# Taking the router of a mixture layer from the first norm and the attended values, with picks in batches

## What is computed

```python
x = x + conv(gn(x))          # rfft over channels, 16 modes, mixed by weights, irfft
t = t + attn(ln(t))          # one head, causal, W_q, W_k, W_v, W_o 256 x 256
# ffn(ln(t)):
router_logits = flat_x @ router_w                    # 256 x 8
topk_w, topk_idx = top_k(softmax(router_logits), 2)  # then normalised to sum 1
for e in range(8):
    h = gelu(flat_x @ w_fc[e])                       # 256 x 1024
    out = out + combine[:, e:e+1] * (h @ w_proj[e])  # 1024 x 256
t = t + out
```

## Time and profile before

| | us |
|---|---|
| median of 3 runs | 723.77 (722.03 to 724.03) |
| profiled execution, its own time | 726.27 |
| span from first to last instruction | 724.5 |
| PE busy | 647.4 (89%) |
| DVE busy | 516.5 (71%) |
| POOL busy | 429.6 (59%) |
| ACT busy | 413.7 (57%) |
| mean granted clock of PE | 0.964 of full |

### The profile page before, as it was taken

How to read it: one execution, slowest core, us unless ns; L and a number is a source line. 1 busy time by engine, 2 the same in 40 slices (tenths; PEclk the granted TensorE clock), 3 DMA queues, 4 the chain that set the end, 5 groups by cost and what they waited for, 6 DMA issues and landing times. The chain is left out here.

```text
span 724.5 us, 16522 instructions
## 1 busy us (share of the span) xinstructions
PE 647.4 (89%) x5010; PEld 624.2 (86%) x5010; DVE 516.5 (71%) x1217; ACT 413.7 (57%) x703; POOL 429.6 (59%) x340
## 2 busy tenths in 40 slices
PE   0496999999940699999999999999999999999993
PEld 0385888888840599999999999999999999999993
DVE  8764577777764577787878777877787777777761
ACT  1804777766520556566666656565656565756550
POOL 5002326777666256766666666767676767676763
PEclk9999999999975799999999999999999999999998
DMA  8805752222323454433131313222222222232312
GB/s 343 273 0 186 276 179 74 92 90 97 106 105 113 136 162 146 96 108 59 29 59 31 57 31 57 41 47 45 43 49 39 51 37 52 36 53 35 57 19 29
DMA packets 39486, 64.13 MB, mean 89 GB/s; under 512 B 3808, under 2 KB 34848, under 8 KB 38304
## 3 DMA queue, kind: packets, MB, share of 16 engines
q0 software_dynamic: 14304, 18.92, 14.7%
q1 hardware_dynamic: 14816, 34.55, 13.5%
q10 hardware_dynamic: 10336, 10.31, 5.6%
HBM read 37.96 MB, written 25.81 MB: 88 GB/s over the span
## 5 line engine op out<-in xcount | busy, mean ns | idle before, releaser
L574 POOL TENSOR_TENSOR pj_lo<-w_ffn,pj_hi 128x1024 fp32r<-128x1024 f32 x78 | 189.1, 2425 | 122.8 <-ACT pj_hi L615 106.3
L1167 DVE TENSOR_TENSOR fc_lo<-w_ffn,fc_hi 128x1024 fp32r<-128x1024 f32 x78 | 116.1, 1527 | 86.2 <-ACT fc_hi L615 86.2
L564 POOL DMA_INDIRECT out<-y,add_id x78 | 121.9, 1563 | 45.1 <-issue 43.7
L615 ACT ACTIVATE pj_hi<-w_ffn 128x1024 fp32r x78 | 82.7, 1060 | 94.9 <-PE psO L1464 89.3
L615 ACT ACTIVATE fc_hi<-w_ffn 128x1024 fp32r x78 | 78.3, 1051 | 43.4 <-issue 43.4
L1464 PE MATMUL psP<-pj_hi,h_hi 128*128 128x256 f32 x312 | 91.5, 293 | 0.2 <-DVE h_lo L1167 0.2
L1464 PE MATMUL psP<-pj_hi,h_lo 128*128 128x256 f32 x312 | 88.5, 284 | 0.0
L1464 PE MATMUL psO<-pj_hi,h_lo 128*128 128x256 f32 x312 | 88.3, 283 | 0.0
L1464 PE MATMUL psO<-pj_lo,h_hi 128*128 128x256 f32 x312 | 88.3, 283 | 0.0
L1464 PE MATMUL psP<-pj_lo,h_hi 128*128 128x256 f32 x312 | 88.3, 283 | 0.0
L1464 PE MATMUL psO<-pj_hi,h_hi 128*128 128x256 f32 x312 | 88.1, 282 | 0.0
(11 more groups left out here) (252 smaller groups left out, 1639.4 us busy)
## 6 DMA issues: line engine op xcount, KB each, us to landing
w_ffn<-in_w_ffn SPq DMA_DIRECT2D x8, 2048.0 KB, 8.2
xg<-slots ACTq DMA_DIRECT2D x38, 265.0 KB
xc<-in_x_ch SPq DMA_DIRECT2D x4, 1024.0 KB, 8.9
out<-x SPq DMA_DIRECT2D x16, 256.0 KB
x<-in_x_tok SPq DMA_DIRECT2D x1, 3072.0 KB, 25.2
slots<-fill SPq DMA_DIRECT2D x9, 265.0 KB, 2.8
out<-y,add_id POOLq DMA_INDIRECT x78, 3.9
w_in<-in_w_in SPq DMA_DIRECT2D x1, 1024.0 KB, 13.7
```

The source lines that it names most:

```text
L564: nc.gpsimd.indirect_dma_start(out_d, bass.IndirectOffsetOnAxis(ap=add_id[:, s:s + 1], axis=0), y[:, s, :], None, compute_op=ALU.add).then ...
L574: nc.gpsimd.tensor_tensor(pj_lo[:, 4 * a:4 * a + 4, :], w_ffn[:, bass.ds(e, 1), (2 + a) * DFF:(3 + a) * DFF].rearrange("p a (c d) -> p (a ...
L615: nc.scalar.activation(out, src, ACT.Copy, **kw).then_inc(done, 1)
L1167: v.tensor_tensor(out, whole, upper.bitcast(F32), ALU.subtract).then_inc(done, 1)
```

## The change

It touches the opening, the attention stage and one input; the experts' stage stays as it is.

- **Router.** The second norm's input is x1 + attn, and the logits are linear in it up to the root. So `router_w`, with its column means taken away (`route_w`), is kept in 8 extra columns of `vo_w`, and its product with `vo_w` in 8 more (`riders`). The value products then have 272 columns: the attended values' product with 264 of them yields the attention part of the logits, and the last 8, times the root of variance of the first norm (`roots[..., 4:6]`, power 0.5), the part of x1 (`ride_in`). `logits_in` adds both. The logits are then right up to the factor of the second norm's reciprocal root, which changes no pick; `gap_scale` multiplies the difference of the two best by it before the exponential. The transposes of the second norm, ACT's copy of them (`router_in`) and `route` are gone.
- **Picks** go in batches of 4, 4, 2, 2, 2, 2 sequences, 8 or 4 tiles. The running count over tiles is one scan (`tensor_tensor_scan`) over expert-major columns in place of a chain of additions. `count_before` writes columns 384 on of `psP`.
- **Order.** Slots run from -2. The inverse DFT and `conv_out` run two sequences ahead; both norms of a slot share one variance, one root and one shift step, and the second norm's statistics and rows come one slot later. `shifts` of the slot before opens each DVE slot. POOL issues up to five scatters before the root of its slot (all that are ready from slot 16 on). ACT splits the upper parts of `spec` for two sequences at once, DVE the lower; `xn_t` and `v_b` have two buffers; the xn transposes use `psG`.
- **Opening.** Both folds, the column sums and a transposition of `vo_w` come before the first inverse DFT.

The diff, cut to its core: changed buffer declarations, slices by batch size, renamed semaphores and nearly all removed lines are left out (the removed ones stand in the functions above).

```diff
-PAIRS = B // 2
-EARLY_PAIRS = PAIRS - 2
-PT = NT // PAIRS
+BATCHES = (0, 4), (4, 4), (8, 2), (10, 2), (12, 2), (14, 2)
+BT = 2 * max(n for _, n in BATCHES)
+EARLY = 12
+RIDE = 2 * E
+VW = D + RIDE
+WHERE = 3 * P
...
+SLOTS = B + 6
...
+        def norms_in(k):
+            return (0 if on(k - 2) else 2), (4 if on(k + 2) else 2)
...
-            for k in range(-1, B + 6):
+            for k in range(-2, SLOTS - 2):
...
+            def root(k):
+                first, end = norms_in(k)
+                end += 2 if end == 4 else 0
+                pool.wait_ge(var_ready, k + 3)
+                nc.gpsimd.tensor_tensor(roots[:, k + 2, first:end], ve[:, first:end], power[:, first:end],
+                                        ALU.pow).then_inc(roots_ready, 1)
             def scatter(b, s, n):
+                j, t = batch_of(b), 2 * b + s
                 pool.wait_ge(xn2_ready, t + 1)
                 pool.wait_ge(weights_ready, j + 1)
                 pool.wait_ge(slot_ready, j + 1)
                 gate()
                 nc.gpsimd.indirect_dma_start(
+                    slots_d, bass.IndirectOffsetOnAxis(ap=slot[:, n, t:t + 1], axis=0), rows[:, t, :],
+                    None).then_inc(scattered_early if b < EARLY else scattered_ending, 16)
+            left = [(b, s, n) for b in range(B) for s in range(2) for n in range(PICKS)]
             def pool_slot(k):
+                room = 5 if k < B else len(left)
+                while left and room and k >= sum(BATCHES[batch_of(left[0][0])]) + 2:
+                    scatter(*left.pop(0))
+                    room -= 1
+                if on(k - 2) or on(k + 2):
+                    root(k)
...
-            for n, (w, bank) in enumerate(((qk_w, psS), (vo_w, psP))):
+            for n, (w, bank) in enumerate(((vo_w, psT1), (qk_w, psG))):
...
             def values(b):
                 act.wait_ge(v_mm, b + 1)
+                if b > 1:
+                    act.wait_ge(pv_mm, b - 1)
+                    act.wait_ge(ride_read, b - 1)
+                for s, bank in enumerate((psV, psT2)):
+                    copy(v_b[b % 2][:, s, :], bank[:, 0:VW], v_ready)
...
-                act.wait_ge(gap_ready, j + 1)
+                act.wait_ge(gap_scaled, j + 1)
...
+            def upper_spec(p):
+                if p > 1:
+                    act.wait_ge(idft_mm, 2 * p - 2)
+                this = spec[:, p * 2 * SEQ:(p + 1) * 2 * SEQ]
+                copy(spec_parts[0:MC, p % 2, :], this, spec_upper)
+                copy(spec_parts[MC:2 * MC, p % 2, :], this, spec_upper)
...
             def act_slot(k):
                 if on(k - 1):
                     softmax(k - 1)
+                for j in batch_at(k - 3):
                     pick_ratio(j)
                 if on(k):
                     keys_in(k)
+                if on(k + 1):
+                    if later(k + 1):
+                        act.wait_ge(t1_mm, k + 1)
+                    normalise(k + 1, k, 2, xn, xn_ready)
                 if on(k - 1):
                     probs_out(k - 1)
                 if on(k):
                     values(k)
                 if on(k + 1):
                     normed_in(k + 1)
+                if on(k - 3):
+                    normalise(k - 3, k, 0, rows[:, 2 * k - 6:2 * k - 4, :], xn2_ready)
+                if k % 2 == 0 and on(k + 4):
+                    upper_spec(k // 2 + 2)
+            act.wait_ge(vot_mm, 1)
+            copy(g_t[:, :, :], psT2[:, :], vot_ready)
+            act.wait_ge(spec_ready, WI)
+            upper_spec(0)
+            act.wait_ge(ride_mm, 1)
+            nc.scalar.activation(vo_w[:, :, D:D + E], psT1[:, 0:DH * E].rearrange("p (h e) -> p h e", h=DH),
+                                 ACT.Copy).then_inc(ride_ready, 1)
             run_attention(act, act_slot)
...
+            def variances(k):
+                first, end = norms_in(k)
+                dve.wait_ge(stats_ready, sum(on(n - 2) + on(n + 2) for n in range(-2, k + 1)))
+                for n in range(first, end):
                     ins = v.bn_aggr(mv[:, n, :], st[:, n, :])
+                ins.then_inc(mv_ready, 1)
+                dve.wait_ge(mv_ready, k + 3)
+                ins = v.tensor_scalar(ve[:, first:end], mv[:, first:end, 1], LN_EPS, None, ALU.add)
+                if end == 4:
+                    ins = v.tensor_scalar(ve[:, 4:6], mv[:, 2:4, 1], LN_EPS, None, ALU.add)
+                ins.then_inc(var_ready, 1)
+            def shifts(k):
+                first, end = norms_in(k)
+                dve.wait_ge(roots_ready, k + 3)
+                v.scalar_tensor_tensor(shift[:, k + 2, first:end], mv[:, first:end, 0], -1.0, roots[:, k + 2, first:end],
+                                       ALU.mult, ALU.mult).then_inc(shift_ready, 1)
...
+            def ride_in(b):
+                dve.wait_ge(v_ready, 2 * b + 2)
+                v.tensor_tensor(ride[:, :, :], v_b[b % 2][:, :, D + E:VW], wide(roots[:, b, 4:6]), ALU.mult).then_inc(ride_read, 1)
+            def logits_in(b):
+                dve.wait_ge(ride_read, b + 1)
+                at = 2 * (b - BATCHES[batch_of(b)][0])
+                for s, bank in enumerate((psO, psT1)):
+                    ins = v.scalar_tensor_tensor(logits[:, at + s, :], bank[:, D:D + E], rinv[:, s:s + 1], ride[:, s, :],
+                                                 ALU.mult, ALU.add)
+                ins.then_inc(logits_ready, 1)
...
+            def gap_scale(j):
+                b, n = BATCHES[j]
+                dve.wait_ge(gap_ready, j + 1)
+                dve.wait_ge(roots_ready, b + n + 4)
+                a = gap[:, 0:2 * n].rearrange("p (b s) -> p b s", s=2)
+                v.tensor_tensor(a, a, roots[:, b + 4:b + n + 4, 0:2], ALU.mult).then_inc(gap_scaled, 1)
...
+                v.tensor_tensor(picked[:, 0:t, :], hot[:, 0, 0:t], hot[:, 1, 0:t], ALU.add)
+                v.tensor_copy(shifted_in[:, :, 0], carry[:, :])
+                then(v.tensor_tensor(shifted_in[:, :, 1:t], hot[:, 0, 0:t - 1].rearrange("p t e -> p e t"),
+                                     hot[:, 1, 0:t - 1].rearrange("p t e -> p e t"), ALU.add))
+                v.tensor_tensor_scan(before[:, 0:size], inside[t][:, :], shifted[:, 0:size], 0.0, ALU.mult,
+                                     ALU.add).then_inc(before_ready, 1)
...
+            def lower_spec(p):
+                dve.wait_ge(spec_upper, 2 * p + 2)
+                if p > 1:
+                    dve.wait_ge(idft_mm, 2 * p - 2)
+                this = spec[:, p * 2 * SEQ:(p + 1) * 2 * SEQ]
+                v.tensor_tensor(spec_parts[2 * MC:, p % 2, :], this, spec_parts[0:MC, p % 2, :].bitcast(F32),
+                                ALU.subtract).then_inc(spec_lower, 1)
             def dve_slot(k):
+                if on(k - 3) or on(k + 1):
+                    shifts(k - 1)
+                if on(k - 2):
+                    alone(x2_ready, 2 * k - 2)
+                    statistics(k - 2, 0)
+                for j in batch_at(k - 2):
+                    pick(j)
+                    count_picks(j)
+                for j in batch_at(k - 3):
+                    gap_scale(j)
+                    find_slots(j)
+                    if BATCHES[j][0] == EARLY:
+                        need_of_first()
+                    weigh(j)
                 if on(k - 1):
                     sums_inverse(k - 1)
-                        if j == EARLY_PAIRS:
+                    ride_in(k - 1)
+                if (k + 2) * 2 == NT // 4:
+                    dve.wait_ge(ld_x[1], 16)
+                if on(k + 2):
+                    conv_out(k + 2)
+                    alone(x1_ready, k + 3)
+                    statistics(k + 2, 2)
+                if on(k - 2) or on(k + 2):
+                    variances(k)
                 if on(k - 1):
                     attn_out(k - 1)
                 if on(k):
                     highest(k)
                 if on(k - 1):
+                    logits_in(k - 1)
+                if k % 2 == 0 and on(k + 4):
+                    lower_spec(k // 2 + 2)
...
             def attend(b):
                 pe.wait_ge(pt_ready, b + 1)
+                pe.wait_ge(v_ready, 2 * b + 2)
                 if later(b):
+                    pe.wait_ge(logits_ready, b)
+                here = v_b[b % 2][:, :, 0:D + E]
+                mm(psO[:, 0:D + E], p_t[:, 0:P], here[:, 0, :], start=True, stop=True)
+                mm(psT1[:, 0:D + E], p_t[:, P:2 * P], here[:, 0, :], start=True, stop=False)
+                mm(psT1[:, 0:D + E], p_t[:, 2 * P:3 * P], here[:, 1, :], start=False, stop=True).then_inc(pv_mm, 1)
             def pe_slot(k):
-                    fold(wv, wo_t, psP)
                 if on(k):
                     query_keys(k)
+                    values(k)
                 if on(k - 1):
                     probs_t(k - 1)
+                if on(k + 2):
+                    idft_of(k + 2)
+                if k == -2:
+                    riders()
+                if on(k + 1):
```

(34 more changed lines are left out.)

418 lines of the change are left out of this document (158 added, 260 removed).

## The result

Seven runs of each kernel, on one chip: before 723.04 us (721.16 to 724.03), after 725.88 us (724.55 to 727.20), ratio 1.0044 with a 95% interval of 1.0031 to 1.0057. The profiled execution of the changed kernel took 725.07, its span is 723.2; the profiled one of the kernel before took 726.27 (span 724.5), more than any of the seven runs beside which the change was timed. W is the time at which the last weights of the picks are written.

A forecast was written before the change was run, and what follows sets the result against it. PE's instruction stream was taken to bound the attention stage, with a serial tail after it. Opening +2.7, tail +3.2 and slots -5.7 summed to +0.2 us: forecast 724.0, own range 720.5 to 728, over all cases 715.5 to 731.5.

The forecast's parts named there:

- PE, removed and added: Attention slots: PE loses 1.24 us per slot and gains small additions; a plain slot takes 7.65 us.
- DVE becomes uneven: Attention stage: DVE needs 5.4 us in plain slots, picks add 3.3 or 3.65, finds 2.3 or 2.7, stretching slots.
- POOL's queue: Attention slots: roots behind up to five scatters end 4.2 us into slots 7 and 11, which last 8.85 and 9.3.
- rival 3: Attention stage: PE's clock falls after idle time, 1.2 us in each of six slots, giving 731; chance 0.05.
- The rule on shared access: POOL's scatters: blocked during DVE's two-port copies, three runs would cost 3.6 us more; left out, scatters kept 1.26 apart.
- Opening: Before slot 2: folds ahead of the first inverse DFT make slot 2 start 2.7 us late, bounds 1 to 4.
- Tail: Slot 15's start to W: last pick waits for a root behind eight scatters; 31.1 us, a loss of 3.2.
- The eight-expert stage should keep its length from W on; if it does not, the forecast is wrong for a reason not in it.: Sign to check after the picks' last weights: the unedited expert stage only moves with W, predicted at 503.5 us.
- Rival 1: Attention stage: DVE and ACT keep up, slots 2 to 14 take 101.2 us, total 716.5 (720 if half); chance 0.33.
- Rival 2: Attention stage: DVE bounds from slot 5, nothing won; slots take 114.5 us, total 729.7 or 732; chance 0.24.

The follow-up runs named there:

- the second profiles: Both kernels profiled again unchanged: the kernel before took 730.0 us in that execution; the changed kernel, rerun in another set, 737.65 us, ratio 1.0099 to the kernel before.
- the last experiment: Kernel before with only SP's eight fills waiting for the cast they read instead of the whole plan: 721.26 us, ratio 0.9962 to the kernel before.
- the root between scatters: Changed kernel with POOL issuing two scatters, root, two scatters per slot to 15 instead of five scatters and root: 727.4 us, ratio 0.9978 to the kernel before.
- small one first: Changed kernel with POOL's root ahead of all scatters in slots 16 and 17 only: 733.78 us, ratio 1.0067 to the kernel before.
- the new tail order of the second set: Changed kernel with two scatters, root, two scatters to slot 15, then POOL ordered by readiness: 723.25 us, ratio 0.9898; with the opening reordered too, 720.39 us, 0.9859.

## Why the prediction came out as it did

The forecast was 724.0 with a range of 715.5 to 731.5, and 725.88 lies in it; its sum was +0.2 us, the measured difference +2.8. The forecast's mechanism (PE saves, the opening, POOL's queue and the tail give it back) is what the runs show. The chances gave "faster" 0.41, "within 0.3%" 0.22 and "slower than 726" 0.37. Measured beside the kernel before it is slower, clear of noise, though 725.88 itself lies just under the 726. That the number came so close is in part luck: W is 3.6 later than forecast, and the stretch behind it 5.1 shorter than the profile it was taken from.

- **PE, removed and added.** Right: 7.60 a plain slot for 7.65, and with 1.24 us given back a plain slot lasts 8.93 and the kernel 6 to 10 us longer.
- **DVE becomes uneven.** The mechanism was right, its size too large: slots 10 and 12 took 8.51 and 8.87 where the text had 9.35 and 9.8, slots 5 and 6 8.00 and 8.30 for 8.1 and 8.8. DVE's pieces were somewhat overpriced: start to start, the plain ones add up to 5.0 in slot 6, not 5.4, and gap scaling, finding and weighing of 8 tiles to 2.5, not 2.7.
- **POOL's queue.** The term that was mis-sized most. "One 0.72 less per slot" priced the root by the two-column row; the new root has six columns and takes 1.34, 0.6 more. The first scatter started 0.96 behind the weights in slot 6 and 0.8 in slot 10, and these two slots were 0.5 and 0.8 shorter than forecast, so that what ran past their end reached further into the next. The root ended 5.9 into slot 7 and 5.5 into slot 11, not 4.2 (and the text's own terms, 5.6 + 6.3 + 0.7 - 8.8, give 3.8). The rest of slot 7 then took 5.0 behind the transposes instead of 3.3, since PE, idle for 3.02, ran at a granted clock of 0.56 from 129.4 to 133.3, its lower level for most of it: that is rival 3, priced at 1.2 in each of six slots; it came in one, for about 1.7 us. By the Trainium skill (TensorE: Matmul & The Clock Gate, "What's actually happening") a PE that has been little busy is slowed. Slot 7 agrees; in slot 11 PE was idle 2.69 before the same transposes, and the clock stayed at 1.00. Slot 7: 12.35 for 8.85; slot 11: 10.70 for 9.3.
- Slots 2 to 14 together were 110.8 for 108.8; the errors of the last two points partly cancel.
- **The rule on shared access.** By the Trainium skill (SBUF — State Buffer, "SBUF: two separate sides") a scatter's descriptors cannot be written while VectorE runs a copy in a two-port mode. No run here shows it: behind the first of a run, scatters stayed 1.27 to 1.28 apart through slots full of DVE work, and the five of slot 6 held the root up by 6.34, for 6.3 without the rule. The copies in these slots are small, though: the one at 167.82, inside a scatter of 0.97 us, took 0.17.
- **Opening.** First sum at 60.54 for 60.6. Behind it, slot 2 was 4.43 late for 2.7: the first sum to the first query-keys took 6.9 for 6.0, with roots of four columns (1.48 and 1.01, not 0.72), and slots 0 and 1 took 15.6 for 14.7, with the first query-keys at the lower clock throughout (3.78 for 1.89, granted clock 0.50 from 67.5 to 71.2; before 3.10, 0.63 from 63.2 to 66.2). That is outside the bounds of 1 to 4.
- **Tail.** 31.0 for 31.1 (the steps as listed add up to 30.9), by the named wait: the last pick at 24.3 behind slot 15's start for 24.1.
- **"The eight-expert stage should keep its length from W on; if it does not, the forecast is wrong for a reason not in it."** So it was: 498.4 for 503.5 (500.8 for 505.6 in the second profiles), all of it ahead of the first down product. W was missed by 3.6 (224.83 for 221.2), and the holes of the profile before were taken for part of the kernel. In the timed runs the loss of 3.85 in W shows as 2.8. That the holes cost the timed runs of the kernel before little, as its profiled execution 3.2 above its median and the last experiment suggest, is argued, not shown.
- **Rivals.** Rival 1's premise, that DVE and ACT keep up, is nearly true: with the root between scatters slots 2 to 14 took 102.5 (84.10 to 186.55), against its 101.2. It failed as a forecast since POOL was not in it. Rival 2 (DVE bound from slot 5 on) is not what happened: with POOL's order alone changed, slots 2 to 14 gained nine tenths of what rival 1 had them gain (12.1 of 13.3).

## What to carry to other kernels

An engine's program that holds both bulk issues and the small operation that others wait for should be written in the order in which its instructions become ready. Both "small one last" and "small one first" stalled here, by 8.6 and 9.8 us (the second with unexplained stalls in it; from the changed kernel's trace some 4.6 can be estimated without them). Ordering by readiness took 14.4 us off within one set; with the opening's order and sooner fills, +0.44% became -2.1%, and the fills alone gave the kernel before 0.4%. Price a small operation at its new size and by the engine it runs on, and when a profile shows gaps within one engine's own dependent chain, look at a second execution before taking them for part of the kernel. When a wait covers more than what the waiting instruction reads (the fills and the whole plan), cut it down: in the kernel before that one line brought 2.4 us.

## What was not expected of the hardware

- GpSimd's power on 128 partitions costs by the column: 0.72 us for two, 1.03 for four in the steady slots, 1.34 for six, some 0.15 to 0.16 per column on 0.4. The first one of four columns took 1.48.
- A dependent instruction of DVE in these chains normally starts 0.03 to 0.04 us behind the end of the one it waits for. In some stretches of 7 to 13 us many start 0.2 to 1.4 us behind: in the plan chain of the kernel before (twice), and in the last pick and count of both kernels with the new tail order of the second set, for example

```profile
210.32 0.19 DVE L1025 TENSOR_TENSOR cand<-cand,attn_in 128x32 f32<-128x32 f32 x1 [0.52 <-DVE cand L1024]
211.05 0.19 DVE L1026 TENSOR_REDUCE key<-cand 128x4 f32<-128x32 f32 x1 [0.54 <-DVE cand L1025]
...
216.73 0.23 DVE L1070 TENSOR_TENSOR_SCAN before<-inside,shifted 128x32 f32<-128x32 f32 x1 [1.04 <-DVE shifted L1068]
```

  POOL issues scatters at the same time in all of these, but it does so in the changed kernel's chain too, which has none. The cause was not found, nor whether the stalls put down to "remote" have the same one.
- A pause of PE of 3.02 us was followed by a granted clock of 0.56 over the next 3.9 us (0.66 in the second profile), one of 2.69 us by no fall (1.00 in both profiles). Each is one place in the program.
